# Decoder of six sublayers on one core: where the first cross attention's masked keys and the constants of two later stages are made

## What is computed

```python
x = _layernorm(x + _L0_attn_ref(x, ...))       # chunked attention: 64 x 64 chunks within 1024 tokens
x = _layernorm(x + _L0_xattn_ref(x, ctx, ...)) # cross attention, 16 heads of depth 16, 64 keys
x = _layernorm(x + _L0_ffn_ref(x, ...))        # linear layer with block-wise 4-bit rounding of x and weight
x = _layernorm(x + _L1_attn_ref(x, ...))       # causal attention with rotary positions, 16 query and 4 key heads
x = _layernorm(x + _L1_xattn_ref(x, ctx, ctx, mask, ...))
x = _layernorm(x + _L1_ffn_ref(x, ...))        # router and 8 experts, two taken for each token
```

## Time and profile before

| | us |
|---|---|
| median of 3 runs | 1342.64 |
| lowest and highest | 1342.58, 1343.19 |
| profiled execution, its time | 1344.01 |
| its span | 1342.3 |
| busy in the span: TensorE, VectorE, ScalarE, GpSimd | 1173.1, 846.0, 789.7, 609.5 |
| chunk stage, about | 2 to 163 |
| first cross attention, about | 164 to 265 |
| quantised layer, about | 262 to 342 |
| causal stage, about | 344 to 966 |

### The profile page before, as it was taken

The page is one execution under the profiler, slowest core; times in us unless marked ns, Lnnn a source line. Parts: engine busy times, 40 slices in busy tenths (PEclk is TensorE's granted clock), DMA queues, the critical chain, the costliest instruction groups (busy, mean ns, idle before and its releaser), DMA issues. The chain is left out here.

```text
span 1342.3 us, 25832 instructions
## 1 busy us (share of the span) xinstructions
PE 1173.1 (87%) x8247; PEld 872.3 (65%) x8248; DVE 846.0 (63%) x1511; ACT 789.7 (59%) x2121; POOL 609.5 (45%) x641
## 2 busy tenths in 40 slices
PE   7888489667799999999989999999899856999991
PEld 4554267455566777777666677777577645888881
DVE  2588789884245555656345556666577658888883
ACT  2488347424556555665555556655367767777773
POOL 1277537647454521431363322310056614888873
PEclk9999779897699999999999999999999857999996
DMA  9100000000110000000100000100190041333334
GB/s 300 49 1 0 0 1 2 1 16 16 29 36 17 17 17 17 17 17 2 32 16 19 15 18 17 48 1 1 30 347 2 1 167 53 55 55 51 55 51 138
DMA packets 42266, 58.03 MB, mean 43 GB/s; under 512 B 6992, under 2 KB 34768, under 8 KB 42160
## 3 DMA queue, kind: packets, MB, share of 16 engines
q1 hardware_dynamic: 34672, 46.44, 11.5%
q0 software_dynamic: 7488, 10.23, 4.7%
HBM read 32.54 MB, written 13.63 MB: 34 GB/s over the span
## 5 line engine op out<-in xcount | busy, mean ns | idle before, releaser
L2100 DVE TENSOR_REDUCE ga_neg_top<-ps 128x1 f32<-128x128 f32 (+7 forms) x256 | 182.1, 753 | 193.8 <-PE ps L1870 193.5
L1990 ACT COPY ga_e_tr<-ps 128x512 f32<-128x512 f32 (+3 forms) x192 | 92.0, 479 | 173.8 <-PE ps L1879 170.9
L1981 ACT ACTIVATE ga_e<-ps,ga_neg_top 128x128 f32<-128x128 f32 (+7 forms) x256 | 188.2, 743 | 7.5 <-DVE ga_neg_top L2100 6.8
L1879 PE MATMUL ps<-ident,ga_e 128*128 128x128 f32 x1152 | 165.2, 278 | 0.9 <-DVE ga_e_tr L2108 0.8
L1895 PE MATMUL ps<-ga_e_tr,ga_v 128*64 128x256 f32 x1152 | 151.7, 391 | 4.1 <-ACT ga_att L1998 4.1
L1879 PEld LDWEIGHTS ps<-ident,ga_e 128*128 128x128 f32 x1152 | 123.3, 142 | 28.1 <-ACT ga_e L1981 14.7
L2108 DVE COPY ga_e_tr<-ps 128x128 f32<-128x128 f32 (+3 forms) x192 | 106.0, 552 | 35.0 <-PE ps L1879 34.7
L2651 DVE TENSOR_TENSOR ex_w_lo<-ex_gate_up,ex_w_hi 128x1024 fp32r<-128x1024 f32 x78 | 95.5, 1225 | 34.0 <-ACT ex_w_hi L2522 32.0
L2055 POOL TENSOR_TENSOR ga_q_lo<-shared,ga_q_hi 128x1024 fp32r<-128x1024 f32 x15 | 35.5, 2368 | 174.9 <-ACT ga_q_hi L1971 174.9
L1895 PEld LDWEIGHTS ps<-ga_e_tr,ga_v 128*64 128x64 f32 x1152 | 72.5, 136 | 48.9 <-issue 23.3
L489 ACT ACTIVATE ca_e<-ps,ca_neg_top 128x64 f32<-128x64 f32 x256 | 76.7, 358 | 36.2 <-DVE ca_neg_top L528 36.2
(11 more groups left out here) (334 smaller groups left out, 2801.3 us busy)
## 6 DMA issues: line engine op xcount, KB each, us to landing
shared<-shared SPq DMA_DIRECT2D x80, 128.0 KB, 2.4
ex_gate_up<-in_ex_gate_up SPq DMA_DIRECT2D x1, 8192.0 KB, 24.4
ex_down<-in_ex_down SPq DMA_DIRECT2D x1, 4096.0 KB, 35.7
x_tr<-in_x_tr SPq DMA_DIRECT2D x4, 512.0 KB, 6.7
x_nat<-in_x SPq DMA_DIRECT2D x1, 2048.0 KB, 11.6
gated_rows<-shared SPq DMA_DIRECT2D x4, 512.0 KB, 4.5
x_tr<-summed_rows SPq DMA_DIRECT2D x8, 256.0 KB, 4.0
out<-x_tr SPq DMA_DIRECT2D x8, 256.0 KB, 2.1
```

Source lines behind the costliest of these rows:

```text
L1879: last = nc.tensor.transpose(ps_tr[n % 2][:, (kb - k0) * P:(kb - k0 + 1) * P], e[half][t % 2][:, kb * P:(kb + 1) * P], core.ident[:])
L1981: nc.scalar.activation(e[half][t % 2][:, 0:blocks(t) * P], ps_scores(t, half), ACT.Exp, bias=neg_top[t % 2][:, half:half + 1], accum_out=s ...
L1990: nc.scalar.copy(e_tr[g % 2][:, k0:k1, half, t % 2 * P:(t % 2 + 1) * P], ps_tr[n % 2][:, 0:(k1 - k0) * P].rearrange("p (k t) -> p k t", t= ...
L2100: nc.vector.tensor_reduce(neg_top[t % 2][:, half:half + 1], ps_scores(t, half), AX.X, ALU.max, negate=True).then_inc(top_ready, 1)
```

## The change

`dve_keys` of the first cross attention moves from the chunk stage's drain to the head of VectorE's program in the next stage, ahead of `dve_values`. The nine instructions of the quantised layer's constants move from behind step 1 of the cross attention into `dve_round`, between the halving of `mx_delta` and the wait for GpSimd's power; their tiles and semaphores belong to `MxWeights` now. `dve_setup` of the causal stage moves from behind step 2 of the cross attention into step t = 1 of the chunk loop, behind the query copy of tile 1 and ahead of the maxima of tile 0. Instructions, shapes and what they wait for stay as they were; what TensorE waits for is only renamed.

```diff
-def stage_chunk_attention(core, mx, prefetch, following):
+def stage_chunk_attention(core, mx, prefetch, front, following):
...
                                                 bq[:].unsqueeze(2).to_broadcast([P, KD, P]), ALU.add).then_inc(q_copied, 1)
+                    if at(t, 1):
+                        front.dve_setup(dve)
                     if u5 is not None:
                         tail.dve_variance(dve, u5)
...
                     if at(u2, TILES - 2):
                         following.dve_context(dve)
-                    if at(u2, TILES - 1):
-                        following.dve_keys(dve)
...
+    def dve_constants(self, dve):
+        nc, ident, parts = self.core.nc, self.core.ident, self.bias_parts
+        dve.wait_ge(self.core.consts_ready, 2)
+        nc.vector.tensor_copy(self.ident_bf[:], ident[:]).then_inc(self.ident_ready, 1)
+        nc.vector.memset(self.ones[:], 1.0)
+        link = Chain(dve, self.bias_step, 0, 6)
+        link(nc.vector.tensor_copy(parts[:, 0], self.bias_row[:]))
+        link(nc.vector.tensor_tensor(self.bias_rest[:], self.bias_row[:], parts[:, 0], ALU.subtract))
+        link(nc.vector.tensor_copy(parts[:, 1], self.bias_rest[:]))
+        link(nc.vector.tensor_tensor(parts[:, 2], self.bias_rest[:], parts[:, 1], ALU.subtract))
+        link(nc.vector.tensor_scalar(self.bias_rows[:], parts[:, 0], ident[:, 0:1], None, ALU.mult))
+        link(nc.vector.scalar_tensor_tensor(self.bias_rows[:], parts[:, 1], ident[:, 1:2], self.bias_rows[:], ALU.mult, ALU.add))
+        nc.vector.scalar_tensor_tensor(self.bias_rows[:], parts[:, 2], ident[:, 2:3], self.bias_rows[:], ALU.mult,
+                                       ALU.add).then_inc(self.bias_ready, 1)
+        link.end()
+
     def dve_round(self, dve):
         nc, blocks = self.core.nc, self.BLOCKS
         dve.wait_ge(self.loaded, 16 * self.loads)
         dve.wait_ge(self.tanh_ready, 1)
         nc.vector.tensor_scalar_mul(self.delta[:], self.delta[:], 0.5).then_inc(self.halved, 1)
+        self.dve_constants(dve)
         dve.wait_ge(self.tweak_ready, 1)
...
-                pe.wait_ge(ident_ready, 1)
+                pe.wait_ge(weights.ident_ready, 1)
...
-                pe.wait_ge(bias_ready, 1)
+                pe.wait_ge(weights.bias_ready, 1)
...
-                def constants():
-                    dve.wait_ge(core.consts_ready, 2)
-                    nc.vector.tensor_copy(ident_bf[:], core.ident[:]).then_inc(ident_ready, 1)
-                    nc.vector.memset(ones[:], 1.0)
...
+                setup.dve_keys(dve)
                 setup.dve_values(dve)
                 dve.wait_ge(weights.tweak_ready, 1)
                 first, begun = quantizer_of(0), 0
                 for step in range(CROSS_STEPS):
                     cross.dve_step(dve, step)
-                    if step == 1:
-                        constants()
-                    if step == 2:
-                        front.dve_setup(dve)
...
-                stage_chunk_attention(core, mx, [cross0, causal, cross1], setup0)
+                stage_chunk_attention(core, mx, [cross0, causal, cross1], front, setup0)
```

More of the change, by code:

```diff
@@ L1136, in __init__ @@
         self.loads = 3
+        self.ident_bf, self.ones = (core.sb(ctx, f"mx_{n}", [P, P], BF16) for n in ("ident", "ones"))
+        self.bias_rows = core.sb(ctx, "mx_bias_rows", [P, D], BF16)
+        self.ident_ready, self.bias_step, self.bias_ready = (core.sem(f"mx_{n}") for n in ("ident_ready", "bias_step", "bias_ready"))
     def begin(self, ctx):
@@ L1145, in begin @@
                                                             for n in ("amax", "power", "inverse", "factor"))
+        self.bias_parts = core.sb(ctx, "mx_bias_parts", [P, 3, D], BF16)
+        self.bias_rest = core.sb(ctx, "mx_bias_rest", [P, D])
     def load(self, sp):
@@ L1480, in stage_cross_then_mxfp4 @@
         xq_tr = [core.sb(ctx, f"mx_xq_tr{i}", [P, KD, P], BF16) for i in range(2)]
-        ident_bf = core.sb(ctx, "mx_ident", [P, P], BF16)
-        bias_parts = core.sb(ctx, "mx_bias_parts", [P, 3, D], BF16)
-        bias_rest = core.sb(ctx, "mx_bias_rest", [P, D])
-        bias_rows = core.sb(ctx, "mx_bias_rows", [P, D], BF16)
-        ones = core.sb(ctx, "mx_ones", [P, P], BF16)
         z = [core.sb(ctx, f"mx_z{i}", [P, D]) for i in range(DEEP)]
@@ L1492, in sem @@
             return core.sem(f"mx_{name}")
-        ident_ready, x_step, xq_ready = sem("ident_ready"), sem("x_step"), sem("xq_ready")
+        x_step, xq_ready = sem("x_step"), sem("xq_ready")
         xq_tr_ready, xq_tr_copied, y_ready = sem("xq_tr_ready"), sem("xq_tr_copied"), sem("y_ready")
-        bias_step, bias_ready, z_ready, stats_ready = sem("bias_step"), sem("bias_ready"), sem("z_ready"), sem("stats_ready")
+        z_ready, stats_ready = sem("z_ready"), sem("stats_ready")
         var_ready, eps_added, rstd_ready, offset_ready = sem("var_ready"), sem("eps_added"), sem("rstd_ready"), sem("offset_ready")
@@ L1561, in project @@
                     need(pe, z_ready, u - 1)
-                    nc.tensor.matmul(ps_y[u % 2], ones[:], bias_rows[:], start=True, stop=False)
+                    nc.tensor.matmul(ps_y[u % 2], weights.ones[:], weights.bias_rows[:], start=True, stop=False)
                     for k in range(KD):
@@ L1574, in _ @@
                         for k in range(KD):
-                            last = nc.tensor.transpose(ps_xq[t % 2][:, k, :], x_q[g % 2][:, i, k * P:(k + 1) * P], ident_bf[:])
+                            last = nc.tensor.transpose(ps_xq[t % 2][:, k, :], x_q[g % 2][:, i, k * P:(k + 1) * P], weights.ident_bf[:])
                         last.then_inc(xq_tr_ready, 1)
@@ L1622, in residual_and_moments @@
                     nc.vector.bn_aggr(mv[i][:], stats[i][:]).then_inc(var_ready, 1)
-                def constants():
-                    dve.wait_ge(core.consts_ready, 2)
-                    nc.vector.tensor_copy(ident_bf[:], core.ident[:]).then_inc(ident_ready, 1)
-                    nc.vector.memset(ones[:], 1.0)
-                    link = Chain(dve, bias_step, 0, 6)
-                    dve.wait_ge(weights.loaded, 16 * weights.loads)
-                    link(nc.vector.tensor_copy(bias_parts[:, 0], weights.bias_row[:]))
-                    link(nc.vector.tensor_tensor(bias_rest[:], weights.bias_row[:], bias_parts[:, 0], ALU.subtract))
-                    link(nc.vector.tensor_copy(bias_parts[:, 1], bias_rest[:]))
-                    link(nc.vector.tensor_tensor(bias_parts[:, 2], bias_rest[:], bias_parts[:, 1], ALU.subtract))
-                    link(nc.vector.tensor_scalar(bias_rows[:], bias_parts[:, 0], core.ident[:, 0:1], None, ALU.mult))
-                    link(nc.vector.scalar_tensor_tensor(bias_rows[:], bias_parts[:, 1], core.ident[:, 1:2], bias_rows[:], ALU.mult, ALU.add))
-                    nc.vector.scalar_tensor_tensor(bias_rows[:], bias_parts[:, 2], core.ident[:, 2:3], bias_rows[:], ALU.mult,
-                                                   ALU.add).then_inc(bias_ready, 1)
-                    link.end()
+                setup.dve_keys(dve)
                 setup.dve_values(dve)
```

## The result

The changed kernel takes 1332.48 us (median of 4 runs, 1331.27 to 1334.26), the kernel before beside it 1342.61 us (4 runs). The ratio is 0.9928, 95% interval 0.9914 to 0.9942, so it is faster by 7.8 to 11.5 us. The profiled execution took 1333.38 us, its span 1331.6 us. Forecast was 1335.8: the sign and the range are right, the gain of 10.1 us is 3.3 us more than the sum of 6.85.

A forecast was written before the change was run, and what follows sets the result against it. VectorE was taken to bound the chunk drain's chain and the first cross stage. The gains 1.85 + 0 + 5.0 - 0 - 0 = 6.85 us, taken from the median 1342.64, gave 1335.8 us; range 1331.5 to 1340.5.

The forecast's parts named there:

- Part 1: Chunk stage's drain: without `dve_keys`, GpSimd's sum of halves is late next; gain 1.85 us, bounds 1.4 and 2.6.
- a residual: Drain: GpSimd's residual could stand in the way of the small `ca_diag` sums for about 0.2 us, at most 0.73.
- Part 2: Head of the first cross stage: `dve_keys` there is covered by the wait for the first query; cost 0.
- Part 3: First cross stage's first tiles, freed of constants and set-up: maximum 4 gains 5.0 us, bounds 3.8 and 5.5.
- The 1.2 us of clock in the sum: First cross stage: without the 2.59 us gap TensorE stays at 2.4 GHz, bringing tile 4 another 1.2 us sooner.
- Rival A: First cross stage: the clock falls again in tiles 2 to 4, gain there only 3.8, time 1337.0 us; chance 0.14.
- D: Cross stage: TensorE keeps the lower clock far in, 3.6 us more per tile, time 1346.7 us; chance 0.06.
- Parts 4 and 5: Constants under GpSimd's power in the front, `dve_setup` under a chunk loop wait: cost 0 each, bounds 0.9 and 0.25.
- Rival B: Front: the constants stand behind GpSimd's power and TensorE loses 0.9 us, time 1336.7 us; chance 0.10.
- the step that forecast nothing behind the head: Behind the cross stage's first tiles: VectorE bounds and the shift is handed on, with no further gain or loss.
- The likeliest case: Whole kernel: the full 6.85 us gain stays to the end, time 1335.8 us; chance 0.52.
- Rival C': Causal stage's start: its stretch at the lower clock becomes shorter by 10 us, time 1331.2 us; chance 0.06.

The follow-up runs named there:

- e1: The kernel before with only `dve_keys` moved to the head of the cross stage; 1339.78 us, ratio 0.9981.
- e8: The changed kernel with `dve_setup` put behind step 8 of the cross attention; 1337.64 us, ratio 0.9972 to the kernel before.
- e10: The changed kernel with unread TensorE products filling gaps at the end of the quantised stage; 1334.08 us, ratio 0.9951 to the kernel before.
- e7: The changed kernel with the nine constants made twice in the front; 1333.79 us, ratio 0.9944 to the kernel before.
- e6: The changed kernel with a pad of idle VectorE work at the chunk stage's end; 1337.50 us, ratio 0.9964 to the kernel before.
- e5: The kernel before with a pad of idle VectorE work at the chunk stage's end, nothing moved; 1346.34 us, ratio 1.0038.
- e2: The kernel before with only the nine constants moved into the front; 1339.94 us, ratio 0.9985.
- e3: The kernel before with only `dve_setup` moved to tile 1 of the chunk loop; 1336.52 us, ratio 0.9956.
- e9: The changed kernel with unread TensorE products filling gaps in the drain and first cross steps; 1333.41 us, ratio 0.9946 to the kernel before.

## Why the prediction was right, and where it was short

- **Part 1, forecast 1.85, measured 2.1** (stage start of e1; 2.45 in the changed kernel, of which 0.3 isn't the keys'). The mechanism is the one foretold; the term was small by the 0.2 us of GpSimd's two instructions, against which the forecast had set a residual that didn't stand in the way. Within its bounds.
- **Part 2, forecast 0: holds.** 1.52 us of keys, done well before the query.
- **Part 3, forecast 5.0, measured 5.5** at maximum 4 and at the sixth (27.46 us from the stage's start, before 32.97). Maximum 2 gained 3.90 against 3.8. The 1.2 us of clock in the sum came true: scores 3 at 1.13. Rival A did not occur; D neither, and tile 2's 1.13 denies it. But the size holds only to about 1 us, and there was luck in it: from stage start to sixth maximum e8, e10, e7 and e6, with the same instructions there, took 27.47, 26.52, 27.93 and 28.68 us, by the tile with which the clock rose, so the same part would have measured between 4.3 and 6.5.
- **Parts 4 and 5, forecast 0: hold within 0.1 us.** The casts at 19.32 and 20.05 kept their length beside the power. Rival B's price was about right (e7: 0.84 lost for a chain 2.7 us late), its condition not met. The Trainium skill (SBUF — State Buffer, section "SBUF: two separate sides") tells of a port pair that either VectorE or GpSimd locks for a whole instruction. By that the gain was to be 0.9 us less; the trace with the 17-column power does not show a lock. Behind GpSimd's long product it does show one: in e8 a VectorE instruction of two columns took 1.13 us and ended at 204.58, GpSimd's product beside it at 204.55. The cast of 1.94 before ended at 180.80, GpSimd's product beside it at 180.71:

```profile
178.81 1.90 POOL L889 TENSOR_TENSOR xa_e<-xa_e,xa_recip 128x1024 f32<-128x1024 f32 x1 [13.83 <-DVE xa_recip L1018]
```

- **Where it fell short is the step that forecast nothing behind the head.** The likeliest case handed the 6.85 us on to the end unchanged; 0.6 us came in the quantised stage, 0.3 further on, 1.9 on the way to the experts and 0.4 behind. Rival C' came nearest, a stretch that spends less time at 1.2 GHz, with a chance of 0.06 and in the wrong place: I named the causal stage's head, which lies 626.7 us ahead of the second cross stage's first maximum before and 626.4 after. That it is the earlier arrival that shortens such a stretch, as C' has it, is not shown. e5 and e6 show that the experts' 1.9 us can go either way; as I had no row on the sign, the range was the place for it, and it held it.

The test set for "wrong" (maximum 4 gaining under 3 us, or the head start changing by over 2 us until the causal stage) was not met: 5.5 us, and 7.99 to 8.62. Nor does the last open part matter to the sign: without the 1.9 us of the two profiled executions, 8.2 of the 10.1 us between the medians are left.

## What to carry to other kernels

Small VectorE work at the head of a pipelined stage costs what the other engines' work doesn't cover (0.6 of 3.03 us for the constants in e2, 2.6 of 3.26 for the set-up in e3, at maximum 2 and counted from the stage's start), and it can cost the clock of the engine that it lets idle. A wait on another engine in an earlier stage is the place for it, and there the slack is what the next engine's free buffers hide (here 1.9 us, measured by doing the work twice). Before speeding up an engine, look whether anyone waits for it: TensorE at twice the clock through the whole drain gained nothing there. And a few us of a single change can come from a later stage of TensorE at the lower clock. Before crediting them to the edit, look whether the old kernel can have the shorter stretch too, and take more than one profile of each; here each kernel has one.

## What the runs showed of the hardware

- The same 60 us stretch with the same work took 59.7, 60.5 or 61.5 us, at a mean granted clock of 0.67 in the shortest and 0.61 in the two others. The shortest and the longest occur both in the old kernel (e5, before) and in the changed one (changed, e6). Executions of one kernel differ too: 1337.79 us at 0.946, 1343.96 us at 0.941.
- In the head of the first cross attention TensorE's clock rose with tile 1 (e10), 2 (changed, e8) or 3 (e6, e7), with the same instructions there. At the lower level a tile's scores take 2.08 us and not 1.13; the sixth maximum came 0.5 to 1.2 us later for each such tile.
- TensorE stayed at 1.2 GHz from just behind 337 us until past 350 while it was busy 12.88 of 13.00 us (e10). With its gaps filled it kept 2.4 GHz in the drain and the cross attention's head (e9).
- A power of 17 columns on GpSimd (3.19 us) let casts and three-operand instructions of VectorE run beside it at their usual lengths (0.23 and 0.48 us). In e8 a power of a single column took 1.44 us and not its usual 0.57 while VectorE made the pick matrix (1.21 us, from 204.83).
